# Layer-0 attention: two weighted sums issued together behind every second pair of scores

## The reference, cut to what matters

```python
# x: (16, 256, 128), 16 heads of 64
q = l2norm(xn @ w_q) * q_scale                    # per head
k = l2norm(concat(null_k, xn @ w_k)) * k_scale    # 2 null keys per head
sim  = 8 * einsum('bhid,bhjd->bhij', q, k) + dist * slopes
sim  = where(causal_mask, -max, sim)
attn = softmax(sim, axis=-1)
out  = einsum('bhij,bhjd->bhid', attn, concat(null_v, v))
return out.reshape(b, n, 1024) @ w_out
```

## Time and profile before

| | us |
|---|---|
| runs (3) | 1049.5, 1047.17, 1043.44 |
| median | 1047.17 |
| span of the profiled execution | 1043.3 |
| PE busy | 961.4 (92%) |
| DVE / POOL / ACT busy | 692.3 / 650.4 / 630.9 |
| layer-0 attention, batches 2 to 5 | about 150 to 309 |
| first experts | about 311 to 397 |
| batches 6 to 15 | about 397 to 795 |

### The profile page before, as it was taken

One profiled execution on the slowest core, in us unless ns is written; L12 is line 12 of the kernel. 1 busy time (PEld: TensorE's weight loads), 2 busy tenths in 40 slices (PEclk: granted clock), 3 DMA queues, 4 the chain that ended last, 5 costly groups with the idle time before them and its releaser, 6 DMA issues.

```text
span 1043.3 us, 21426 instructions
## 1 busy us (share of the span) xinstructions
PE 961.4 (92%) x6330; PEld 690.3 (66%) x6330; DVE 692.3 (66%) x2589; ACT 630.9 (60%) x1945; POOL 650.4 (62%) x803
## 2 busy tenths in 40 slices
PE   5699989999999979999999999999998999999965
PEld 2465546666658976666665665666666788999954
DVE  6988867886673335867768768677885474345634
ACT  4458857667664557677676775766765564444442
POOL 4663787888855544667776678788746651555540
PEclk9889999999999999999999999999999999999997
DMA  9300202202427783033032030331232134787759
GB/s 296 79 7 6 42 27 66 71 26 64 113 74 188 221 233 84 10 72 81 6 66 50 22 71 26 73 67 41 52 82 52 34 102 143 227 229 226 219 168 242
DMA packets 95444, 103.19 MB, mean 99 GB/s; under 512 B 10096, under 2 KB 83031, under 8 KB 95089
## 3 DMA queue, kind: packets, MB, share of 16 engines
q1 hardware_dynamic: 88752, 89.36, 33.5%
q0 software_dynamic: 6592, 12.65, 3.5%
HBM read 77.54 MB, written 23.50 MB: 97 GB/s over the span
## 4 chain that ended last, share of the span: by engine, by line
PE 54%; DVE 18%; ACT 7%; POOL 7%; issue 6%; DMA 3%; SPq 3%; DVEq 0%; POOLq 0%; ACTq 0%
PE bank L1347 9%; PE bank L823 8%; PE bank L834 7%; PE bank L1376 7%; PE bank L1403 5%; DVE arena L2032 5%; PE bank L1391 4%; ACT arena L1759 4%; PE bank L1366 3%; PE bank L1426 3%; DVE arena L2041 3%; POOL arena L1130 2%; DVE arena L1932 2%; POOL expert_rows L655 2%; DMA arena<-in_b 1%
## 5 line engine op out<-in xcount | busy, mean ns | idle before, releaser
L1759 ACT ACTIVATE arena<-arena 128x128 f32<-128x128 f32 (+1 forms) x512 | 226.9, 446 | 96.7 <-DVE arena L2032 96.5
L2032 DVE CUSTOM_DVE_ANT_0 arena<-bank,arena 128x128 f32<-128x128 f32 (+1 forms) x512 | 183.0, 412 | 107.1 <-PE bank L1376 104.4
L1347 PE MATMUL bank<-arena 128*128 128x512 f32 x384 | 211.1, 636 | 6.0 <-ACT arena L1748 3.6
L1130 POOL TENSOR_TENSOR arena<-arena 128x512 f32<-128x512 f32 x128 | 133.4, 1045 | 121.7 <-ACT arena L1735 104.1
L2041 DVE COPY arena<-bank 128x384 f32<-128x384 f32 x256 | 130.0, 549 | 21.1 <-PE bank L1391 20.9
L1145 POOL TENSOR_TENSOR arena<-arena 128x512 f32<-128x512 f32 x128 | 129.5, 1048 | 1.3
L1735 ACT ACTIVATE arena<-bank 128x512 f32<-128x512 f32 x192 | 112.7, 588 | 27.8 <-PE bank L1347 27.5
L1391 PEld LDWEIGHTS bank<-const,arena 128*128 128x128 f32 x768 | 91.3, 142 | 56.0 <-issue 55.0
L784 POOL DMA_INDIRECT expert_out<-arena x71 | 71.1, 1002 | 90.0 <-DVE arena L923 42.1
L1376 PE MATMUL bank<-arena 64*128 64x128 f32 (+1 forms) x1024 | 119.3, 351 | 2.2 <-DVE arena L2032 1.5
L1403 PE MATMUL bank<-arena 128*64 128x256 f32 (+1 forms) x1024 | 112.2, 340 | 9.1 <-DVE arena L2041 8.7
(11 more groups left out here) (304 smaller groups left out, 1634.1 us busy)
## 6 DMA issues: line engine op xcount, KB each, us to landing
arena<-in_wp SPq DMA_DIRECT2D x40, 514.0 KB
arena<-recip_rows SPq DMA_DIRECT2D x30, 512.0 KB, 6.4
XN<-in_wp SPq DMA_DIRECT2D x24, 514.0 KB
arena<-expert_rows SPq DMA_DIRECT2D x46, 129.0 KB, 3.2
arena<-in_b SPq DMA_DIRECT2D x64, 64.0 KB
arena<-expert_out SPq DMA_DIRECT2D x16, 256.0 KB, 5.1
expert_out<-fill SPq DMA_DIRECT2D x11, 338.6 KB, 7.9
expert_rows<-fill SPq DMA_DIRECT2D x1, 2644.5 KB, 21.6
```

Of the source, the lines that this page charges most:

```text
L1130: pool.tensor_tensor(sq[:, i % 2], r, r, ALU.mult).then_inc(S["sq_done"], 1)
L1347: mm = pe.matmul(RING[bnk][:, :], xa[:, p, t * P:(t + 1) * P], wqkv[:, 512 * k:512 * k + 512], start=True, stop=True)
L1759: ins = act.activation(w, w, ACT.Exp, bias=nm[:, p, 16 * t + h:16 * t + h + 1], scale=-1.0, accum_out=den[:, p, 16 * t + h:16 * t + h + 1])
L2032: ins = v.tensor_tensor_reduce(out=SPb[:, c % 2, 384 * k + P * t:384 * k + P * t + n], in0=SBANK[k][:, P * t:P * t + n], in1=alibi[:, h, N ...
```

## The change

In an even step (c = 2, 4, 6) the weighted sums of pairs c-2 and c-1 are both issued behind the scores of pair c+1; in an odd step none. In step 0 the last batch's pairs 6 and 7 come. `finish` issues pairs 6 and 7. The wait for `lg_read` moves to the first place where batch 0 weighs. Scores, transposes and all other engines' code stay.

```diff
-                    if c:
-                        if isinstance(b, int) and b == 0 and c == 1:
+                    if c and c % 2 == 0:
+                        if isinstance(b, int) and b == 0 and c == 2:
                             pe.wait_ge(S["lg_read"], 1)
+                        weigh(b, p, c - 2)
                         weigh(b, p, c - 1)
-                    elif before and not flushed:
+                    elif c == 0 and before and not flushed:
+                        weigh(b - 1, 1 - p, NPAIR - 2)
                         weigh(b - 1, 1 - p, NPAIR - 1)
                     ring(c, 0)
                     turn_p(b, c)
...
             def finish(b, p):
+                weigh(b, p, NPAIR - 2)
                 weigh(b, p, NPAIR - 1)
                 turn_comb(b)
```

## The result

| us | before | changed | ratio, 95% interval |
|---|---|---|---|
| first set, median of 4 and 4 runs | 1047.64 | 1063.11 | 1.0154 [1.0113, 1.0196] |
| the set of E5 to E8 below, 12 and 4 runs | 1045.20 | 1058.39 | 1.0108 [1.0061, 1.0155] |
| span of the profiled execution (first set) | 1043.3 | 1059.0 | |

The change makes the kernel slower by 1.1 to 1.5%. I had said 0.7%, 1045 to 1060 us: the sign was right, the size was half of what came, 7 us against 15.5 in the first set and 13.2 in the other, and 1063 lies outside the range.

A forecast was written before the change was run, and what follows sets the result against it. PE was taken as the bound in steady batches, with POOL or DVE leading elsewhere. Terms 3.5 - 0.1 + 2.0 + 1.1 + 1.2 = 7.7 us, rounded down to +7 on 1047.17, gave 1054 us; 8-in-10 range 1045 to 1060.

The forecast's parts named there:

- One sum out of an odd step, one more in an even step (-0.80, +0.65): On PE, an odd step loses a weighted sum's whole 0.80 us; a second sum in an even step adds 0.65 us.
- Step 1 saves 0: In steady batches unit 0 waits for ACT's chain from the step's scores, so PE's 0.80 us becomes waiting; saved 0.
- Step 3 saves 0.50: In steady batches the second transposes have 0.55 us slack against ACT's emptying; 0.50 us saved, 0.30 a new wait.
- steps 5 and 7 save 0.80: In steady batches no wait was near enough to bind in these steps, so each saves the whole 0.80 us.
- Batches 0 to 5: First attention part: batches 0 and 1 lose +0.6 us each, batches 2 to 5 0.50 each; 3.2 us in all.
- Batch 6 begins behind the expert stage, ... about -0.1: In batch 6 the sums of pair 6 move into finish and fill a wait; about -0.1 us.
- Batches 7 to 9: 0.50 each: Batches 7 to 9 counted as steady, even steps paying 2.60 us and odd steps saving 2.10; +0.50 us each.
- Batches 11 to 13, +0.65 each through POOL: From 597 to 745 us POOL waits for ACT's copy of unit 1, 0.65 us later per batch; 2.0 us in all.
- Batch 14, 0.6: Step 0 stalls on DVE and hides its 0.65 us, steps 1 and 3 save nothing; +0.6 us.
- PE does not take all: Rival over the whole kernel: PE is the bound and saves all 9.6 us, 1037.6; chance 0.1 with its half-way form, 1046.
- paid back in the stretches of DVE and POOL: Rival: where DVE and POOL bind, earlier probabilities in odd steps return the costs; near +2 us, 1049; chance 0.2.
- The third rival: Odd steps run into DVE's row maxima, or step 2 delays POOL every batch; 0.65 us more in 10 batches, 1060; chance 0.1.

The follow-up runs named there:

- E5: The changed kernel, unmodified, run again on another chip for a second trace and reference; ratio to before 1.0108.
- E8: Only the sums of pairs 0 and 1 issued together, in step 2, all others one by one; 1056.32 us against 1045.20 before, ratio 1.0109.
- E1: The changed kernel with ACT emptying the first transposed q/k block ahead of the exponentials in steps 1 and 3; 1066.62 us against 1069.03 of before, ratio 0.9988.
- E2: The kernel before, one sum per step, with ACT emptying the first transposed q/k block ahead of the exponentials in steps 1 and 3; ratio to before 1.0001.
- E7: The changed kernel with one extra unread GpSimd multiplication ahead of the normalise in steps 7 to 10 of GpSimd's program; 1058.64 us, ratio to before 1.0117.
- E10: The changed kernel with the sums of pairs 0 and 1 one by one again, the other three couples of pairs together; ratio to before 1.0007.
- E4: The changed kernel with 14 unread identity transposes on PE ahead of three waits of about 2 us; 1080.77 us against 1069.03 of before, ratio 1.0114.
- E9: Sums together and ACT's first q/k block emptied ahead of exponentials (steps 1, 3) in batches 0 to 5 only, the rest as before; ratio to before 0.9983.
- E6: The kernel before, unmodified, run again on another chip for a second trace; 1044.76 us, a single run.

## Why the prediction was half right

The forecast was 7 us (7.7 before rounding), 15.7 and 14.1 came in the two pairs of traces. The prices of the sums and the steady batches were right; the step that failed is the one that carried the steady batch's figures into the stretches where DVE leads: batches 7 to 9 (1.5 forecast, 3.7 and 3.7 measured), 10 (0.3; 0.7 and 1.6), 14 (0.6; 1.9 and 2.0), and the end of the first part with batch 6 (-0.1; 2.8 and 1.6).

- **One sum out of an odd step, one more in an even step (-0.80, +0.65): right**, 1.45 us for two in a row and 0.65 us in each of steps 0, 2, 4 and 6 of a steady batch.
- **Step 1 saves 0, because ACT's chain hangs on the scores: right**, 5.03 and 5.03, and shown by E1 (0.63 of the 0.80 us come as soon as ACT's order lets them) and by E2 as its control.
- **Step 3 saves 0.50: 0.39.** The second block of transposes starts 0.13 us behind the end of ACT's emptying in the changed kernel (253.21 and 253.08), not the 0.05 that were taken for the semaphore's way; **steps 5 and 7 save 0.80: right**. The steady batch is +0.60 instead of +0.50, 39.31 to 39.91.
- **Batches 0 to 5: 3.2 forecast, 3.7 and 2.4 in two pairs of traces.** Right in sum by luck, since not in its parts: batch 1 lost 2.5 us (43.06 to 45.59), batch 0 won 1.0 to 1.5. In batch 1 step 3 took 5.72 instead of 4.59 us, in E8 too, and 4.2 with ACT's new order.
- **"Batch 6 begins behind the expert stage, ... about -0.1": wrong, +0.9 to +2.1 for the stage and +0.7 for the batch.** The transposes of comb (L1416) at the end of the first part come 0.6 us late (6.94 instead of 6.35 us behind the last scores), since the second of the multiplications that feed them meets POOL's normalise (1.03 instead of 0.31 us), in every trace in which pairs 4 and 5 stand together and in no other. I had the sums fill a wait there and left DVE out. The rest differs from run to run (92.2 to 92.8 before, 93.7 to 94.3 changed). Batch 6 has no sum in its step 0 and pays 0.65 three times for 0.48 and 0.80 saved in steps 3 and 5, +0.67, which my own prices would have given.
- **"Batches 7 to 9: 0.50 each": wrong, 1.0, 1.35, 1.35.** This is the plainest case of the step that failed. I took batches 7 to 9 for steady ones because PE is nearly full in them. But DVE is the bound there from step 7 to step 1, and its chain got 0.7 us longer by being held. E7 gives that back in batches 8 and 9 and leaves 0.64 each. In batch 7 no multiplication is held; by E8 and E10 its 1.0 is 0.65 for pairs 0 and 1 and 0.36 for the others.
- **Batches 11 to 13, +0.65 each through POOL: right in sum by accident.** 0.60, -0.1 to 0.4, 1.7. In batch 13 step 7 takes 5.9 us in both kernels: scores 1 wait for DVE's row maxima, so nothing is saved there, while step 0 pays. That POOL's wait for unit 1 makes the +0.65, as I had it, no run shows.

```profile
703.54 0.93 PE L1376 MATMUL bank<-arena 64*128 64x128 f32 x8 [0.92 <-DVE arena L2035]
```

- **Batch 14, 0.6: wrong, 1.9 and 2.0.** I had step 0 hide its 0.65 in a stall on DVE. In both traces of the changed kernel both multiplications are held there, 2.08 us instead of 1.18 (changed, then before), and step 0 takes 6.68 and 6.59 us instead of 5.69:

```profile
749.99 2.08 DVE L2061 TENSOR_TENSOR arena<-arena 128x32 f32<-128x32 f32 x2
```
```profile
735.47 1.18 DVE L2058 TENSOR_TENSOR arena<-arena 128x32 f32<-128x32 f32 x2
```

In E4 only one is held and step 0 takes 5.69 us, as before. In E9, whose batches 6 to 15 are issued as before, both are, and it takes 6.52: the second hold comes and goes with the two engines' timing and is not the change's alone.

- **Rivals.** PE does not take all; nothing was paid back in the stretches of DVE and POOL, they cost more. The third rival, 1060, came nearest. Its first half is in the traces: the short steps run into DVE's row maxima, for which the scores wait 8.2 us instead of 1.5, in step 0 of batches 1, 2, 12, 13 and 14. Most of it is the 8.7 us for which the sums waited for DVE before, now ahead of the scores. Its second half, POOL delayed by step 2 in every batch, is not shown. What it lacks is that DVE and POOL exclude each other.

By E8 and E10 the effects are nearly additive: pairs 0 and 1 alone make 1.0109, the other three pairs 1.0007. Within the intervals the pair in step 2 is the whole loss, since it is the one pair whose odd step can save nothing. In E10 the other three pairs gain 2.5 us in batches 0 to 5 (244.1 against 246.6) and lose 1.7 in batches 7 to 14, nearly all of it by the holds in batches 8 and 9 (this leaves out 1.9 us in step 6 of batch 14, where that chip's traces are long whatever the kernel). The 1.1 us of step 3 in batch 1 need both causes: in the changed kernel and E8 two small DVE operations take 1.1 us each beside POOL just ahead of the row maxima, and the step takes 5.72; in E10 one does (1.19) and it takes 4.51; in E1 three do (1.0 to 1.2), but ACT empties the bank first, and it takes 4.21.

## What to carry to other kernels

Taking work out of a step of the fullest engine pays only if what comes next in that step does not hang on another engine's chain from the step's own start; here 0.05 us of slack told it beforehand, and a changed order on the other engine took the loss in step 1 away and gave 0.4 us in step 3. Steps that look alike in the busy shares can be bound by different engines: check in each stretch what the next scores wait for before a term is multiplied by a number of batches. And where two engines can exclude each other, a shift of some 0.45 us in their relative position (POOL's normalise 0.34 us behind the start of DVE's second multiplication before, 0.10 ahead of it changed) is a term of its own, which the order of neither shows.

## What the runs showed of the hardware

- A small DVE multiplication with both inputs in SBUF (128x32, 0.18 us alone) that meets a POOL TENSOR_TENSOR ends with it: 0.31 us beside one of 0.37 us, 1.03 beside one of 1.04 to 1.09, and 2.08 us for a pair in which each meets one. Longer than 0.6 us were 5 of the 32 single records of L2058 before and 9 of the 32 of L2061 in the changed kernel. The DVE row maxima and the copies out of PSUM ran beside the same POOL operations at their usual 0.34 and 0.55 us. The Trainium skill, "SBUF — State Buffer", section "SBUF: two separate sides", describes this: the port pair that both engines use is an exclusive lock for a whole instruction, and a DVE operation with two SBUF inputs needs it against a GpSimd operation that reads SBUF. The traces agree, with 0.18 turned into 1.03 us. By that rule the collision could have been looked for in the trace of before, where it stands at batches 2, 10, 12 and 14.
- The sum of held time says little. In batches 7 to 14 all DVE operations that took 0.2 us or more over their shortest length took 12.3 us over it before (11.8 in E6) and 13.6 changed (15.7 in E5). Before, five of them were a step of the null scores, which is down to two in the changed kernel; the multiplications on the way to the next scores took their place (4.0 and 3.0 us before, 6.9 and 7.8 changed).
- Some single PE waits of about 2 us were followed by a stretch at half the clock, in batches 12 and 14 in one trace of the same kernel and not in the next. It showed as 1.5 us in batch 2 (45.40 and 45.39 us in the changed kernel and E7, 43.85 and 43.88 without it in E5 and E4) and as nothing in batch 14 (38.35 and 38.36 us), where DVE was busy 9 of 10 us.
- The kernel before took 1069.03 and 1070.71 us in two sets and 1044.53 to 1047.64 in the others; nearly all of it is the part behind the first layer's attention. No run here looks into it.
